# Products that nobody reads, placed where TensorE waits: in the tail of attention and ahead of key-ordered scores

## The chip, the core and the metric

The kernel runs on one core of one Trainium2 chip. The metric is device time in microseconds of one launch, weights in device memory at its start. Engines are named as in the profile: PE (TensorE; PEld is its weight load), DVE (VectorE), ACT (ScalarE), POOL (GpSimd), SP (SyncE, which issues most DMAs).

## What is computed

Two layers, each of gated cross-attention and a gated mixture of experts, on x of 8 x 256 rows of 256 values, with a context of 8 x 120 rows. Each layer has 16 heads of 16, and 8 experts of which every row takes two. Layer 0 has experts of three matrices (hidden width 688, SiLU gate), layer 1 of two (width 256, squared ReLU).

```python
x = x + tanh(g_xattn[l]) * attention_l(layernorm(x), ctx)      # softmax over 120 keys
x = x + tanh(g_ffn[l])   * experts_l(layernorm(x))             # top 2 of 8, weighted
# experts of layer 0: (silu(x @ gate[e]) * (x @ up[e])) @ down[e]
# experts of layer 1: square(relu(x @ w1[e])) @ w2[e]
```

## The kernel before

All engines have instruction lists of their own, written out by hand, and meet at semaphores; each list runs strictly in its order. So a product stands where the code puts it on PE, and what is queued behind it waits with it.

**Attention** of a layer goes over 16 units of 128 query rows (`for u in range(NU)`, two units per batch entry; `at(u)` gives the entry `b`, whether u is even, and whether there is a next entry). PE's list of unit u: `scores(G + 1)` are the query-ordered scores of the next unit (L1254), which DVE reduces to row maxima (L841). Then `shifted(G)`, the key-ordered scores of this unit: L1265, with the row maxima subtracted by the products of L1270. ACT exponentiates them (L647 or L649). Ahead of `shifted(G)` stands a wait for `d_ct`, DVE's transpose of the unit before (L858), since both use bank 4 of PSUM. Then follow `route` (L1312: router logits of an earlier unit), `out_proj` (L1299 and the bias L1300), in even units the query projection of the next entry (L1237), in odd units the transposes of the rows after it (L1231) and `ranks` (L1319 to L1328: each row's place among its expert's rows), `max_t` (L1279), `values` (L1291), and `x2_t` (L1306: transposes of normalized rows for the router).

DVE's `residual` (L875) waits for `out_proj`, and makes the statistics; POOL turns them into mean and reciprocal root (`ln2_rstd`, L514 to L519); ACT applies them (L657); PE transposes the result (L1306); ACT copies it (L663); PE makes the logits. DVE takes the top two (`route1`), PE ranks them, DVE makes the row addresses (`route2`), and POOL scatters the rows to device memory, four indirect DMAs per entry (L544). POOL's list mixes `ln2_rstd` and `scatter`, so that a later statistic waits for the scatters ahead of it.

**The last unit** (u = 15) has no next unit's scores; **the tail** is what then remains: the last two transposes for the router, one output projection, two `ranks`, three `route`.

**The expert stage** goes over 39 blocks of 128 rows. SP loads each block (L398) once the list of full blocks is made (`d_l1`) and the scatters of the first six entries have landed (L402). PE transposes a block (`block_t`, L1468), DVE copies it (L1118), PE multiplies it by the first matrices (`up`, L1482), and after the activation transposes the hidden rows (L1495, L1503) and multiplies by the last matrix (`down`, L1512). POOL scatters the results (L551). Block 0's transposes stand on PE behind the last `ranks`. At the very end DVE combines the results without PE.

The added product reads two constants, `ident_b` (a 128 x 128 identity in bf16) and `sel_rows` (128 x 480 in bf16), and writes bank 7 or 2 of PSUM, which are written anew before they are read next.

Of the kernel before, what the change touches and what calls it, by code (L numbers as in the profile page):

```python
# [27 lines left out]
def need(eng, sem, value):  # L28

    if not isinstance(value, int) or value > 0:  # L30
        eng.wait_ge(sem, value)
# [11 lines left out]
def flamingo_kernel(nc, x, ctx_rows, mask, g_xattn, g_ffn, attn_w, attn_b, router_w, experts, out):  # L43
    NB, S, D = x.shape
    K = ctx_rows.shape[1]
# [6 lines left out]
    NU = NT  # L52
# [22 lines left out]
    with es:  # L75
        def sb(name, shape, dt=F32):
            return es.enter_context(nc.sbuf_tensor(name, shape, dt))
# [122 lines left out]
        sel_rows = sb("sel_rows", [P, 4, K], BF16)  # L200
        ident_b = sb("ident_b", [P, P], BF16)
# [11 lines left out]
        ps = es.enter_context(nc.psum_tensor("ps", [P, 8, 512], F32))  # L213
# [92 lines left out]
        def at(u):  # L306
            return u // 2, u % 2 == 0, u // 2 + 1 < NB

        def run_blocks(l, step):
            for j in range(BLOCKS):  # L310
                step(j, j % U3, j == 0, j == BLOCKS - 1)
# [888 lines left out]
        def _(t):  # L1200
            t.wait_ge(C_id, 2)

            for l in range(2):
# [37 lines left out]
                def scores(G):  # L1241

                    b, qt, f = G % NU // 2, G % 2, G // 2 % 2
                    t.wait_ge(a_q, G // 2 + 1)
                    t.wait_ge(a_k, 4 * l + 2 * (b // 4) + 2)
                    if l == 0:
                        for g in range(4):
                            rows = slice(Q4 * g, Q4 * g + Q4)
                            t.matmul(ps[:, g, 0:4 * K].rearrange("p (j k) -> p j k", j=4), ones[rows, :],
                                     mask3[rows, b:b + 1, :].to_broadcast([Q4, 4, K]), start=True, stop=False)  # L1250
                    for j in range(4):
                        for g in range(4):
                            rows = slice(Q4 * g, Q4 * g + Q4)
                            i = t.matmul(ps[:, g, j * K:(j + 1) * K], qT[rows, f, j // 2, j % 2, qt * P:(qt + 1) * P],  # L1254
                                         kT_all[rows, b, j // 2, :], start=(l == 1), stop=(l == 1 or j == 3))
                    i.then_inc(p_s, 1)
# [17 lines left out]
                def max_t(G):  # L1274

                    for h in range(2):
                        t.wait_ge(d_max[h], G + 1)
                    t.wait_ge(d_part, 2 * G + 2)
                    t.matmul(ps[:, 0, 0:P], m_hi, ident_b[:, :], start=True, stop=True).then_inc(p_m, 1)  # L1279
# [16 lines left out]
                def out_proj(G):  # L1296
                    t.wait_ge(d_c, G + 1)
                    for k in range(KT):
                        t.matmul(ps[:, 1, 0:D], cT[:, G % 2, k, :], w_att[:, 3, k, :], start=(k == 0), stop=False)  # L1299
                    t.matmul(ps[:, 1, 0:D], ones[:, :], bo_rows[:, :], start=False, stop=True).then_inc(p_o, 1)  # L1300

                def x2_t(G):
                    t.wait_ge(a_xn2, G + 1)
                    need(t, a_x2, G)
                    for k in range(KT):
                        i = t.transpose(ps[:, 6, k * P:(k + 1) * P], xn2[:, G % 6, k * P:(k + 1) * P], ident[:, :])  # L1306
                    i.then_inc(p_x2, 1)

                def route(G, bank):
                    t.wait_ge(a_x2, G + 1)  # L1310
                    for k in range(KT):
                        i = t.matmul(ps[:, bank, 2 * P:2 * P + NE], xn2T[:, k, :], wr[:, l, k, :], start=(k == 0), stop=(k == KT - 1))  # L1312
                    i.then_inc(p_lg, 1)

                def ranks(B):

                    t.wait_ge(d_mask, B + 1)
                    need(t, d_cum, 2 * B)
                    t.matmul(ps[:, 3, 0:NE], tri[:, :], maskb[:, 0, :], start=True, stop=False)  # L1319
                    t.matmul(ps[:, 3, 0:NE], ones[:, :], cumb[:, :], start=False, stop=True)  # L1320
                    t.matmul(ps[:, 3, NE:2 * NE], tri[:, :], maskb[:, 1, :], start=True, stop=False)
                    t.matmul(ps[:, 3, NE:2 * NE], ones[:, :], maskb[:, 0, :], start=False, stop=False)
                    i = t.matmul(ps[:, 3, NE:2 * NE], ones[:, :], cumb[:, :], start=False, stop=True)
                    if B % NB in (EARLY - 1, NB - 1):

                        t.matmul(ps[:, 3, 2 * NE:3 * NE], ones[:, :], cumb[:, :], start=True, stop=False)
                        t.matmul(ps[:, 3, 2 * NE:3 * NE], ones[:, :], maskb[:, 0, :], start=False, stop=False)
                        i = t.matmul(ps[:, 3, 2 * NE:3 * NE], ones[:, :], maskb[:, 1, :], start=False, stop=True)  # L1328
                    i.then_inc(p_rk, 1)


                B0, G0 = NB * l, NU * l
                if l == 0:
                    ctx_t(0)
# [55 lines left out]
                for u in range(NU):  # L1390
                    b, even, nxt = at(u)
                    B, G = B0 + b, G0 + u
                    if u + 1 < NU:

                        t.wait_ge(a_m, G + 1)
                        if u >= 2:
                            t.wait_ge(d_o, G - 1)
                        if u >= 4:
                            t.wait_ge(d_lg, G - 3)
                        t.wait_ge(a_xnT, min(B + 2, B0 + NB))  # L1400
                        if even and b >= 3:
                            t.wait_ge(d_rk, B - 2)
                        scores(G + 1)

                    if u >= 1:
                        t.wait_ge(d_ct, G)
                    if u >= 3:
                        t.wait_ge(a_x2, G - 2)
                    if l == 0 and u == 0:
                        t.wait_ge(a_ctx, 4)  # L1410
                        t.wait_ge(d_v, 2)
                    if l == 1 and u == 0:
                        t.wait_ge(d_v, 2 * NB)
                    if l == 0 and u - 1 in FILL_V:
                        t.wait_ge(d_v, FILL_V[u - 1] + 1)
                    if l == 0 and u - 1 in (2, 3):
                        t.wait_ge(a_k, u)
                    shifted(G)
                    if u + 1 < NU:
                        t.wait_ge(d_max[0], G + 2)  # L1420
                    if u >= 3:
                        route(G - 3, 1)
                    if u >= 1:
                        out_proj(G - 1)
                    if u + 1 < NU:
                        t.wait_ge(d_max[1], G + 2)
                    if even and nxt:
                        q_proj(B + 1, 0, 2)
                    if not even and b + 2 < NB:
                        x_t(B + 2, 2)  # L1430
                    if not even and b >= 2:
                        ranks(B - 2)
                    if u + 1 < NU:
                        max_t(G + 1)
                    values(G, 0)
                    if even and nxt:
                        q_proj(B + 1, 1, 3)
                    values(G, 1)
                    if u >= 2:
                        x2_t(G - 2)  # L1440
                    if l == 0 and u in FILL_V:
                        v_proj(B0 + FILL_V[u], 5)
                    if l == 0 and u in (2, 3):
                        k_proj(1, u - 2)
                G1, B1 = G0 + NU - 1, B0 + NB - 1
                route(G1 - 2, 5)
                x2_t(G1 - 1)
                t.wait_ge(d_o, G1)
                t.wait_ge(d_lg, G1 - 2)
                out_proj(G1)  # L1450
                t.wait_ge(d_rk, B1 - 1)
                ranks(B1 - 1)
                route(G1 - 1, 7)
                x2_t(G1)
                route(G1, 0)
                t.wait_ge(d_rk, B1)
                ranks(B1)


                t.wait_ge(d_lg, NU * (l + 1))  # L1460
# [3 lines left out]
                def block_t(j):  # L1464
                    t.wait_ge(L_xg[j % U3], 16 * (uses(l, j) + 1))
                    need(t, e_x, J0[l] + j)
                    for k in range(KT):
                        i = t.transpose(ps[:, 7, k * P:(k + 1) * P], xg[:, j % U3, k * P:(k + 1) * P], ident[:, :])  # L1468
                    i.then_inc(b_x, 1)
# [80 lines left out]
                        down(j, offs[j])  # L1550

                block_t(0)
                run_blocks(l, (blk0, blk1)[l])


# [33 lines left out]
```

## Time and profile before

| | us |
|---|---|
| median of 3 runs | 766.17 |
| lowest and highest | 762.58, 766.7 |
| the profiled execution's own time | 769.0 |
| its span, first to last instruction | 767.3 |
| PE busy in the span | 678.0 (88%) |
| DVE busy | 415.0 (54%) |
| ACT busy | 274.4 (36%) |
| POOL busy | 214.4 (28%) |
| mean granted clock of PE in the span | 0.952 |

Layer 0's attention ends about 154 us into the span, its expert stage runs to about 487, layer 1's attention from there to about 640, its expert stage to about 745. A busy PE may be a slow PE: the granted clock tells at which level it worked, 1.00 for 2.4 GHz and 0.50 for 1.2 GHz.

### The profile page before, as it was taken

How to read it: one execution, taken by the hardware profiler on the slowest of the kernel's cores; microseconds unless marked ns; L12 is line 12 of the kernel's file. 1: busy time of each engine (PE TensorE's matmuls, PEld its weight loads, DVE VectorE, ACT ScalarE, POOL GpSimd, SP SyncE). 2: the span in 40 equal slices, each digit the busy share in tenths (PEclk: the TensorE clock that was granted, in tenths of full speed). 3: DMA queues.
4: the chain of work that ended last, by engine and by line, in shares of the span. 5: the costliest groups of instructions: out<-in, count | busy, mean ns of one | idle time of the engine just before them, and what ended most of it. 6: DMA issues, size and time to landing. Idle time of an engine off the chain costs nothing.

```text
span 767.3 us, 17444 instructions
## 1 busy us (share of the span) xinstructions
PE 678.0 (88%) x5804; PEld 520.4 (68%) x5804; DVE 415.0 (54%) x1385; ACT 274.4 (36%) x528; POOL 214.4 (28%) x399
## 2 busy tenths in 40 slices
PE   5798999859999999999999999978888885999970
PEld 3666767637777777777777777657666663788850
DVE  4777888753333333233332332469989876454426
ACT  3556576411211112112111112256555541354530
POOL 4122553460111111111111011212355436344440
PEclk9999999859999999999999999999999986899995
DMA  9044554461131131111011010320112122544428
GB/s 218 18 144 138 182 179 141 148 220 43 56 101 51 36 79 35 35 32 39 28 35 36 29 28 21 143 92 29 58 64 70 64 85 78 151 125 121 123 83 328
DMA packets 50856, 70.71 MB, mean 92 GB/s; under 512 B 7687, under 2 KB 38023, under 8 KB 50771
## 3 DMA queue, kind: packets, MB, share of 16 engines
q1 hardware_dynamic: 42380, 50.85, 22.1%
q0 software_dynamic: 6816, 18.69, 6.9%
q8 instruction: 51, 0.84, 0.5%
q10 hardware_dynamic: 1575, 0.05, 0.1%
q14 instruction: 34, 0.28, 0.1%
HBM read 46.55 MB, written 23.02 MB: 91 GB/s over the span
## 4 chain that ended last, share of the span: by engine, by line
PE 69%; DVE 18%; issue 5%; DMA 4%; POOL 2%; ACT 2%; DVEq 0%; SPq 0%; POOLq 0%; ACTq 0%
PE ps L1482 28%; PE ps L1512 17%; PE ps L1299 4%; DVE m_rows L841 4%; PE ps L1495 3%; DVE x_sb L825 3%; PE ps L1312 2%; PE ps L1237 2%; DVE ctx_q L858 2%; PE ps L1468 2%; PE ps L1291 2%; DMA ys_dram<-share,dest_i 2%; PE ps L1265 2%; PE ps L1254 1%; DVE x_sb L875 1%
## 5 line engine op out<-in xcount | busy, mean ns | idle before, releaser
L1482 PE MATMUL ps<-w_all,share 128*128 x780 | 232.4, 446 | 4.2 <-DVE share L1118 4.2
L1482 PEld LDWEIGHTS ps<-w_all,share 128*128 128x128 f32 x780 | 146.9, 193 | 66.5 <-issue 8.4
L551 POOL DMA_INDIRECT ys_dram<-share,dest_i x78 | 75.9, 974 | 333.2 <-DVE share L1129 279.8
L1512 PE MATMUL ps<-w_all,share 112*128 (+1 forms) x624 | 147.9, 380 | 1.7 <-ACT share L737 1.0
L1512 PEld LDWEIGHTS ps<-w_all,share 112*128 112x128 f32 (+1 forms) x624 | 112.4, 190 | 15.1 <-issue 2.6
L1145 DVE TENSOR_TENSOR share<-share,ps 128x344 f32<-128x344 f32 x78 | 40.0, 513 | 140.5 <-PE ps L1482 79.3
L726 ACT COPY share<-ps 128x512 f32<-128x512 f32 x39 | 22.9, 587 | 151.9 <-PE ps L1495 151.9
L841 DVE TENSOR_REDUCE m_rows<-ps 128x8 f32<-128x960 f32 x64 | 70.4, 1139 | 11.0 <-PE ps L1254 10.9
L723 ACT ACTIVATE share<-ps 128x344 f32<-128x344 f32 x78 | 35.9, 460 | 106.9 <-PE ps L1482 106.9
L544 POOL DMA_INDIRECT xs_dram<-xn,slot_now x64 | 63.7, 996 | 21.9 <-issue 14.6
L514 POOL TENSOR_SCALAR nm<-mv 128x1 f32<-128x1 f32 (+1 forms) x48 | 12.4, 257 | 162.7 <-DVE mv L881 116.8
L1129 DVE COPY share<-ps 128x256 f32<-128x256 f32 x39 | 16.6, 426 | 68.3 <-PE ps L1512 68.3
L1265 PE MATMUL ps<-q_flat,w_all 32*120 32x256 f32 x512 | 42.1, 413 | 8.2 <-DVE ctx_q L858 6.2
L647 ACT ACTIVATE share<-ps,mask_col 120x1024 f32<-120x1024 f32 x32 | 33.9, 1111 | 26.1 <-PE ps L1270 26.0
L1299 PE MATMUL ps<-w_att,cT 128*128 128x256 f32 x128 | 39.8, 438 | 1.4 <-DVE m_rows L841 0.9
L1115 DVE SCALAR_TENSOR_TENSOR xid<-share,be 128x1 f32<-128x1 f32 x78 | 17.3, 222 | 42.4 <-PE ps L1468 42.0
L1254 PE MATMUL ps<-w_all,q_flat 32*128 32x120 f32 x1024 | 35.6, 275 | 4.9 <-ACT q_flat L629 4.2
L1254 PEld LDWEIGHTS ps<-w_all,q_flat 32*128 32x128 f32 x1024 | 33.1, 186 | 8.3 <-issue 6.6
L1237 PE MATMUL ps<-share,w_att 128*128 128x256 f32 x128 | 34.3, 393 | 3.4 <-issue 2.5
L649 ACT ACTIVATE share<-ps 120x1024 f32<-120x1024 f32 x32 | 31.0, 1020 | 14.3 <-PE ps L1270 14.3
L629 ACT ACTIVATE q_flat<-ps,bq,qs 128x256 f32<-128x256 f32 x64 | 32.5, 565 | 8.9 <-PE ps L1237 8.8
L1468 PEld LDWEIGHTS ps<-ident,share 128*128 128x128 f32 x156 | 22.5, 146 | 15.8 <-issue 2.6
(202 smaller groups left out, 991.3 us busy)
## 6 DMA issues: line engine op xcount, KB each, us to landing
share<-xs_dram SPq DMA_DIRECT2D x78, 129.0 KB, 2.1
w_all<-ys_dram SPq DMA_DIRECT2D x16, 512.0 KB, 7.2
w_all<-gate SPq DMA_DIRECT2D x8, 688.0 KB
w_all<-up SPq DMA_DIRECT2D x8, 688.0 KB
w_all<-down SPq DMA_DIRECT2D x8, 560.0 KB
w_all<-w SPq DMA_DIRECT2D x16, 256.0 KB
xs_dram<-q_flat SPq DMA_DIRECT2D x17, 129.0 KB, 2.4
out<-x_sb SPq DMA_DIRECT2D x8, 256.0 KB, 5.6
```

The costliest lines, as they stand in the source:

```text
L544: g.indirect_dma_start(xs_dram, bass.IndirectOffsetOnAxis(ap=slot_now[:, B % 2, t, k:k + 1], axis=0), xn2[:, s + t, :], None).then_inc(sca ...
L551: g.indirect_dma_start(ys_dram, bass.IndirectOffsetOnAxis(ap=dest_i[:, u:u + 1], axis=0), y_sb[:, u, :], None).then_inc(D_y[u], 16)
L723: a.activation(act_sb[:, 344 * q:344 * q + 344], ps[:, 2 * q, 0:344], ACT.Silu).then_inc(e_act, 1)
L841: v.tensor_reduce(m_part[:, 2 * h:2 * h + 2, 0:4], ps[:, 2 * h:2 * h + 2, 0:4 * K].rearrange("p g (j k) -> p g j k", j=4), X, ALU.max).the ...
L1145: v.tensor_tensor(h_sb[:, 344 * q:344 * q + 344], act_sb[:, 344 * q:344 * q + 344], ps[:, 2 * q + 1, 0:344], ALU.mult).then_inc(e_h, 1)
L1237: i = t.matmul(ps[:, bank, 0:S], w_att[:, 0, k, m * P:(m + 1) * P], xn1T[:, k, :], start=(k == 0), stop=(k == KT - 1))
L1254: i = t.matmul(ps[:, g, j * K:(j + 1) * K], qT[rows, f, j // 2, j % 2, qt * P:(qt + 1) * P], kT_all[rows, b, j // 2, :], start=(l == 1), s ...
L1265: t.matmul(ps[0:K, 4 + g, 2 * m * P:2 * (m + 1) * P].rearrange("p (e q) -> p e q", e=2), kT_all[rows, b, m, :], qT[rows, f, m, :, qt * P:( ...
L1299: t.matmul(ps[:, 1, 0:D], cT[:, G % 2, k, :], w_att[:, 3, k, :], start=(k == 0), stop=False)
L1468: i = t.transpose(ps[:, 7, k * P:(k + 1) * P], xg[:, j % U3, k * P:(k + 1) * P], ident[:, :])
L1482: i = t.matmul(ps[:, bank, 0:w], xgT[:, k, :], w_all[:, bass.ds(off + (k * UPW[l] + col - EW[l]), w)], start=(k == 0), stop=(k == KT - 1))
L1512: i = t.matmul(ps[:, 6, 0:D], hT[0:r, c + KD[1] * (j % 2) * l, :], w_all[0:r, bass.ds(off + (KT * UPW[l] + c * D - EW[l]), D)], start=(c = ...
```

## The change

A helper `idle_products(n, bank)` issues n products whose result nobody reads. It is called in the last unit of both layers (six, ahead of the wait for `d_ct`), in layer 1's even units from u = 2 (two at the same place), at eight places of each layer's tail, and between block 0's transposes and its first expert products. The helper waits for nothing and raises no semaphore. Nothing is taken away.

```diff
+                def idle_products(n, bank):
+                    for _ in range(n):
+                        t.matmul(ps[:, bank, 0:4 * K], ident_b[:, :], sel_rows[:, :, :].rearrange("p j k -> p (j k)"),
+                                 start=True, stop=True)
...
                         scores(G + 1)
 
+                    if u == NU - 1:
+                        idle_products(6, 7)
+                    elif l == 1 and even and u >= 2:
+                        idle_products(2, 7)
                     if u >= 1:
                         t.wait_ge(d_ct, G)
...
                 G1, B1 = G0 + NU - 1, B0 + NB - 1
+                idle_products(2, 2)
                 route(G1 - 2, 5)
+                idle_products(3, 2)
                 x2_t(G1 - 1)
                 t.wait_ge(d_o, G1)
                 t.wait_ge(d_lg, G1 - 2)
+                idle_products(1, 2)
                 out_proj(G1)
                 t.wait_ge(d_rk, B1 - 1)
                 ranks(B1 - 1)
                 route(G1 - 1, 7)
+                idle_products(15, 2)
                 x2_t(G1)
+                idle_products(2, 2)
                 route(G1, 0)
                 t.wait_ge(d_rk, B1)
+                idle_products(6, 2)
                 ranks(B1)
+                idle_products(5, 2)
...
                 block_t(0)
+                idle_products(3, 2)
                 run_blocks(l, (blk0, blk1)[l])
```

PE's list at the last unit and the tail of layer 1 (layer 0's reads the same). L1335 is the added product; L1306 transposes normalized rows, L1312 makes logits, L1265 and L1270 are key-ordered scores, L1299 and L1300 the output projection.

```order
 L1291 MATMUL ps<-share,w_all 32x128 x16
 L1306 MATMUL ps<-ident,xn 128x128 x2
+L1335 MATMUL ps<-sel_rows,ident_b 128x480 x6
 L1265 MATMUL ps<-q_flat,w_all 120x256 x4
 L1270 MATMUL ps<-share,sel_rows 120x128 x8
```

```order
-L1306 MATMUL ps<-ident,xn 128x128 x2
-L1312 MATMUL ps<-wr,share 128x8 x2
+L1335 MATMUL ps<-sel_rows,ident_b 128x480 x15
+L1306 MATMUL ps<-ident,xn 128x128 x2
+L1335 MATMUL ps<-sel_rows,ident_b 128x480 x2
+L1312 MATMUL ps<-wr,share 128x8 x2
+L1335 MATMUL ps<-sel_rows,ident_b 128x480 x6
 L1319 MATMUL ps<-maskb,tri 128x8
 L1320 MATMUL ps<-cumb,ones 128x8
```

The first piece puts six products between the transposes that end unit 14 and the last unit's key-ordered scores. In the second the pair L1306, L1312 stands as before, with 15 products ahead of it, 2 within and 6 behind it, ahead of the last `ranks`.

PE's list in an even unit of layer 1 (L1254 are the query-ordered scores of the next unit):

```order
 L1306 MATMUL ps<-ident,xn 128x128 x2
 L1254 MATMUL ps<-w_all,q_flat 128x120 x16
+L1335 MATMUL ps<-sel_rows,ident_b 128x480 x2
 L1265 MATMUL ps<-q_flat,w_all 120x256 x4
 L1270 MATMUL ps<-share,sel_rows 120x128 x8
```

Two products come between the two kinds of scores. The lists of DVE, ACT and SP are the same as before, and POOL's too.

## Rows read from the trace of the kernel before

**Rows 1.** The page, section 2: granted clock in 40 equal slices, tenths.

```profile
PEclk9999999859999999999999999999999986899995
```

**Rows 2.** Windows, engine PE: stretch, length, PE busy (instructions), granted clock, DMA share, GB/s.

```profile
144.00:150.70 6.70, 6.63 (x65) 0.50 0.02 5
...
563.80:567.10 3.30, 1.77 (x37) 1.00 0.02 5
...
580.80:584.20 3.40, 2.13 (x59) 1.00 0.02 5
...
625.20:628.60 3.40, 1.66 (x39) 1.00 0.72 232
...
635.50:642.20 6.70, 3.63 (x34) 1.00 0.18 63
642.30:659.30 17.00, 10.55 (x37) 0.50 0.46 131
```

**Rows 3.** Timeline, PE, units 13 and 14 of layer 1: start, duration, operation [idle before].

```profile
617.26 1.11 PE L1299 MATMUL ps<-w_att,cT 128*128 128x256 f32 x4
...
618.21 0.27 PE L1300 MATMUL ps<-bo_rows,ones 128*128 128x256 bf16 x1
...
621.16 0.71 PE L1265 MATMUL ps<-q_flat,w_all 32*120 32x256 f32 x8
...
622.28 0.29 PE L1270 MATMUL ps<-share,sel_rows 32*120 32x128 bf16 x8
```

**Rows 4.** Timeline, PE, unit 15 of layer 1.

```profile
628.41 1.06 PE L1265 MATMUL ps<-q_flat,w_all 32*120 32x256 f32 x8 [1.74 <-DVE ctx_q L858]
...
630.77 1.02 PE L1312 MATMUL ps<-wr,share 128*128 128x8 f32 x4
...
631.65 2.05 PE L1299 MATMUL ps<-w_att,cT 128*128 128x256 f32 x4
...
633.49 0.42 PE L1300 MATMUL ps<-bo_rows,ones 128*128 128x256 bf16 x1
```

**Rows 5.** Timeline, PE, L1312 in units of layer 1: odd, even, odd, even.

```profile
584.45 0.61 PE L1312 MATMUL ps<-wr,share 128*128 128x8 f32 x4 [0.86 <-DVE m_rows L841]
...
591.08 0.61 PE L1312 MATMUL ps<-wr,share 128*128 128x8 f32 x4 [0.71 <-DVE m_rows L841]
...
600.73 0.61 PE L1312 MATMUL ps<-wr,share 128*128 128x8 f32 x4 [0.86 <-DVE m_rows L841]
...
608.80 0.61 PE L1312 MATMUL ps<-wr,share 128*128 128x8 f32 x4 [0.59 <-DVE m_rows L841]
```

**Rows 6.** Groups of instructions by form: busy, mean ns | idle before.

```profile
L1249 PE MATMUL ps<-mask,ones 32*128 32x480 bf16 x64 | 6.1, 370 | 4.0 <-ACT share L621 1.5 <-ACT q_flat L629 1.2 <-ACT share L637 0.6
```

**Rows 7.** Timeline, PE, tail and first blocks of layer 1.

```profile
644.40 0.69 PE L1306 MATMUL ps<-ident,xn 128*128 128x128 f32 x2 [4.27 <-ACT xn L657]
...
645.54 1.02 PE L1312 MATMUL ps<-wr,share 128*128 128x8 f32 x4 [0.46 <-ACT share L663]
...
648.20 0.17 PE L1319 MATMUL ps<-maskb,tri 128*128 128x8 bf16 x1 [1.63 <-issue]
...
648.97 0.66 PE L1468 MATMUL ps<-ident,share 128*128 128x128 f32 x2 [0.41 <-issue]
...
650.43 2.07 PE L1482 MATMUL ps<-w_all,share 128*128 x4 [0.80 <-DVE share L1118]
...
660.36 1.03 PE L1482 MATMUL ps<-w_all,share 128*128 x4
...
662.52 1.03 PE L1482 MATMUL ps<-w_all,share 128*128 x4
```

**Rows 8.** Layer 0: a piece of the chain that ended last, then PE's timeline.

```profile
157.00 5.26 DMA xs_dram<-xn,slot_now
...
165.85 0.66 PE L1468 MATMUL ps<-ident,share 128*128 128x128 f32 x2 [1.52 <-DMA share<-xs_dram]
...
167.33 6.82 PE L1482 MATMUL ps<-w_all,share 128*128 x16 [0.81 <-DVE share L1118]
```

## The prediction

> **What bounds the kernel now.** I read the page first: its line of granted clock is 9s except at a few slices [rows 1], in a span of 767.3 us. The profiled execution's own time is 769.0 us, 2.8 us above the median of 766.17. PE works 88% of the span, so the question is at which level of its clock. The windows view over both layers gives the answer [rows 2]. From 144.0 to 150.7 the granted clock is 0.50 (1.2 GHz instead of 2.4), and PE is busy 6.63 us of 6.70: this is the last unit of layer 0's attention. Unit 15 of layer 1 runs the same way [rows 4]. Each layer also has a stretch of 17 us at 0.50 from the attention's tail into the first expert blocks: layer 1's row is here, layer 0's shows in rows 8. Ahead of the fall at 628.6, PE was busy 1.66 us of 3.40. Two short falls lie in odd units of layer 1. Ahead of one PE was busy 1.77 us of 3.30; in the next odd unit, with the same operations and 2.13 of 3.40, nothing fell [rows 2]. So the clock falls behind stretches in which PE waited much, and of units that are alike one is hit and another not.
>
> **What a fall costs.** Units 13 and 14 of layer 1 run at the full level [rows 3], unit 15 at half [rows 4]. Key-ordered scores: 621.16 to 622.57, 1.41 us, against 628.41 to 630.77, 2.4 us: 1.0. Router product L1312: 0.61 [rows 5] against 1.02: 0.4. Output projection L1299: 1.11 against 2.05: 0.9. Bias L1300: 0.27 against 0.42: 0.15. Together **2.5 us**, and nothing hides them: VectorE's residual waits for L1300, and from it go statistics, POOL's reciprocal root and POOL's four scatters, whose end sets when the last normalized rows reach PE. A short fall costs, from one L1312 to the next, 608.80-600.73 = 8.07 against 591.08-584.45 = 6.63: 1.4 us [rows 5].
>
> **The change part by part.** It adds 100 products and removes nothing: 12 in the last units, 14 in layer 1's even units, 74 in the two tails. All other engines keep their order. Each streams 480 bf16 columns. No row shows one back to back. L1249 has the same width and type, 370 ns on average [rows 6]; L1300 with 256 columns takes 0.27 [rows 3]. The difference is 0.10 us per 224 columns, or 0.45 ns a column, so 480 cost 0.21 us each where products are pipelined. That is the low end; the high end is 0.37 us each, if nothing overlaps. I take 0.21, since four L1299 of 256 f32 columns start 0.95 us ahead of what follows [rows 3], so PE does pipeline. At half clock it is some 0.4.
>
> *Last unit, six ahead of L1265.* 6 x 0.21 = 1.3 us in an idle of 1.74 [rows 4]: hidden. The products then stand in most of the idle that lies ahead of the fall, so I take it that the unit stays at full speed: **-2.5** in layer 1, and the same taken for layer 0, whose stretch is alike.
>
> *Layer 1's even units, two each.* They do not stand in the idle: in an even unit scores and key-ordered scores follow each other. The 0.42 us delay the latter, and the 0.71 us that PE then waits for the row maxima ahead of the L1312 at 591.08 [rows 5] take it up. ScalarE gets its scores 0.4 later, and has time. Cost 0 (0.4 x 7 = 2.9 if that cover is gone). Gain 0 too: the falls come in the odd units, where no product is added.
>
> *Tail.* In layer 1 PE waits 4.27 us for L1306 [rows 7]: fifteen products take 3.15 (5.6 at the high price, 1.3 too long). Two stand in the idle of about half a microsecond ahead of L1312, six (1.3) in the 1.63 ahead of L1319. Five (1.05) stand where only 0.41 was idle ahead of block 0's transposes: PE is 0.6 late there, but VectorE, which copies the block next, still has the routing to end after L1319, so I charge 0.1 and keep 0.6 for the range. Three (0.6) before the first expert products fit in 0.80. One ahead of the last output projection delays it by 0.2; POOL is then still in its scatters, so nothing. With the clock held, L1306 (0.69, about 0.25 less) and L1312 (1.02, 0.4 less) are shorter, and both are on the path. Then the blocks: 650.43 to 660.36 is 9.93 us for three at half clock, and the next takes 662.52-660.36 = 2.16 [rows 7]; 3 x 2.16 = 6.48, so **-3.45**. Layer 1: -2.5 -0.65 +0.1 -3.45 = -6.5.
>
> Layer 0's expert stage begins otherwise: its first block waits for a load, which waits for the scatter's landing, 5.26 us after the issue at 157.00; PE idles 1.52 us for it and starts at 165.85 [rows 8]. That chain starts at the same residual, so it moves by 2.5; the faster L1306 and L1312 bring nothing. The first sixteen expert products start at 167.33 and run at half until 171.2, 3.9 us, of which half is saved: **-1.95**; block 0's transposes save 0.2. Layer 0: -4.65. Five products fill 1.05 of the 1.52 idle.
>
> After this PE is without idle in the expert stages, so what is gained ahead lasts. Sum: -11.15, and +0.5 for small delays where products fill an idle to its end (three before L1306, of 0.6 us). 766.17 - 10.65 = **755.5**. The median run may have fewer short falls than the profiled execution (2 x 1.4 would be its 2.8 us); they stay as they are before and after.
>
> The Trainium skill (TensorE: Matmul & The Clock Gate, Part 1 on the HAM clock gate) says the monitor is free-running against the kernel, so that the same kernel changes level at other places from run to run. The trace agrees in that like odd units differ. By it, each run of before and after has its own number of short falls, 1.4 us each, which widens the range.
>
> **Rivals.**
> 1. *Slower: the products run at half clock.* If they do not hold the clock, fifteen take 6.0 against 4.27: +1.7; two +0.3, six 2.4 against 1.63: +0.8, five 2.0 against 0.41: +1.6, three 1.2 against 0.80: +0.4. That is +4.8 in layer 1 and about +4 in layer 0, where the load hides part: 775. It decides once a product takes over 0.28 us (4.27/15). For: products follow long idle, in which the clock falls today. Against: from 635.5 to 642.2 the clock was at 1.00 [rows 2], and the fifteen begin in that stretch. 0.05.
> 2. *One fall comes back.* Idle is left in the tail: about 1.1 us after the fifteen, and in layer 0 between five products and the load. One of the two block starts is then at half again: 2 to 3.45 given back, 757.5 to 759. 0.16.
> 3. *The gain is taken up later.* If layer 0's scatter landing stays (the DMA queues are busy there with the last expert's weights), 2.5 is lost: 758. If products also cost the high price, another 2 to 3 in the tails: 761. 0.12, of it 0.05 within 0.5%.
> 4. *The even units' products stop the short falls.* Then up to 2.8 more than summed: 753. Against: they stand a unit away from the idle. 0.07.
> 5. *The falls matter less than their stretches.* Only one place may be on the path, -3.5: 763, within 0.5%. 0.02. The Trainium skill (the same page, Part 1) puts the warm-up penalty under 1% of a typical span; by that the gain would end at 7.7 us, 758.5, in the range of the second rival. The terms above, all from rows, come to more than that.
>
> **How the numbers follow.** The forecast has 0.58, own range 753 to 758. With rivals 2, 4 and most of 3 the range is 751 to 762. Over 0.5% faster (about what a measurement of this kernel can tell from no change) is under 762.3: 0.58 + 0.16 + 0.07 + 0.07 = 0.88. Within 0.5%: 0.07. Slower: 0.05.
>
> **What would show it.** Granted clock 1.00 from the start of both last units through the first expert blocks; L1265 of unit 15 in 0.7 us and not 1.06; the new products 0.2 us apart, ending before the waits they stand in; layer 1's first blocks 2.16 us apart; layer 0's first sixteen expert products in 4.63; short falls in odd units still possible, and even units unchanged in length. A stretch at 0.50 behind the fifteen products, or an idle of PE at L1306 that is gone because the products are late, would make it wrong.

## The result and the profile after

| | before | after |
|---|---|---|
| median, us | 765.32 (4 runs) | 756.21 (4 runs) |
| lowest and highest | 762.58, 766.7 | 754.82, 756.57 |
| the profiled execution's own time | 769.0 | 756.57 |
| its span | 767.3 | 754.8 |
| PE busy in the span | 678.0 (88%) | 684.7 (91%) |
| mean granted clock of PE | 0.952 | 0.985 |

The ratio after to before is 0.9865 with a 95% interval of 0.9827 to 0.9902: by it the change is 10.3 us faster (7.5 to 13.2). It is not the quotient of the medians, which lie 9.1 us apart. The measured 756.21 is inside the range, 0.7 us from the forecast, and in the case that had 0.58. (Each layer's 37 products behind the last unit stand at eight places: seven in the tail and the one behind block 0's transposes.)

The page of after, its first line and the line of granted clock that stood in [rows 1]:

```profile
span 754.8 us, 17644 instructions
...
PEclk9999999999999999999999999999999999999995
```

PE is busy 6.7 us more than before in a span that is 12.5 shorter: the products are work, put in time in which PE would mostly have waited. Of the 8s, the 6 and the two 5s of [rows 1] only the 5 at the end is left: DVE's last combination, in which PE has no work.

The windows of after on PE, over both last units, the tails and the first blocks (length, PE busy, granted clock, DMA share, GB/s):

```profile
142.80:144.70 1.90, 1.39 (x8) 1.00 0.64 208
144.70:151.00 6.30, 6.24 (x92) 1.00 0.12 22
151.10:163.10 12.00, 9.82 (x61) 1.00 0.72 246
163.20:170.00 6.80, 6.13 (x25) 1.00 0.60 186
...
575.90:578.70 2.80, 1.85 (x36) 1.00 0.00 0
578.90:582.10 3.20, 3.20 (x19) 0.50 0.05 10
622.20:628.70 6.50, 6.23 (x92) 1.00 0.04 13
628.80:641.30 12.50, 10.38 (x64) 1.00 0.34 107
641.40:648.00 6.60, 5.35 (x28) 1.00 0.61 182
```

The four long stretches at 0.50 of before, two last units and two tails with their first blocks, now read 1.00. One short fall is left, at 578.8, in an odd unit of layer 1, where no product stands.

Layer 1's last unit, its tail and its first blocks, in PE's timeline (start, duration, operation, idle before), against [rows 4, 7]:

```profile
620.39 1.38 PE L1335 MATMUL ps<-sel_rows,ident_b 128*128 128x480 bf16 x6
622.27 0.71 PE L1265 MATMUL ps<-q_flat,w_all 32*120 32x256 f32 x8 [0.51 <-DVE ctx_q L858]
...
624.08 1.11 PE L1299 MATMUL ps<-w_att,cT 128*128 128x256 f32 x4
...
631.33 3.20 PE L1335 MATMUL ps<-sel_rows,ident_b 128*128 128x480 bf16 x15
635.74 0.44 PE L1306 MATMUL ps<-ident,xn 128*128 128x128 f32 x2 [1.21 <-ACT xn L657]
636.01 0.57 PE L1335 MATMUL ps<-sel_rows,ident_b 128*128 128x480 bf16 x2
...
637.10 1.38 PE L1335 MATMUL ps<-sel_rows,ident_b 128*128 128x480 bf16 x6
638.94 0.18 PE L1319 MATMUL ps<-maskb,tri 128*128 128x8 bf16 x1 [0.47 <-DVE maskb L910]
...
639.16 1.17 PE L1335 MATMUL ps<-sel_rows,ident_b 128*128 128x480 bf16 x5
640.17 0.38 PE L1485 MATMUL ps<-ident,share 128*128 128x128 f32 x2
...
641.35 1.13 PE L1499 MATMUL ps<-w_all,share 128*128 x4 [0.19 <-DVE share L1118]
...
643.43 1.13 PE L1499 MATMUL ps<-w_all,share 128*128 x4 [0.73 <-DVE share L1118]
```

(L1485 and L1499 are the transposes of a block and the first expert products, L1468 and L1482 of before.) Read the idles in brackets. The products before L1265 take 1.74 down to 0.51, and those before L1306 4.27 down to 1.21. Fifteen take 3.20, six 1.38, five 1.17. The last of each group's time is what one takes alone, 0.37, so the pitch is (3.20-0.37)/14 = 0.20. L1265 takes 0.71, not 1.06; L1299 1.11, not 2.05. The first expert products of one block and the next stand 2.08 apart, where three blocks took 9.93.

The same in layer 0, where block 0 waits for a load (here L1485 has no wait that the view shows), against [rows 8]:

```profile
161.72 1.17 PE L1335 MATMUL ps<-sel_rows,ident_b 128*128 128x480 bf16 x5
162.95 0.41 PE L1485 MATMUL ps<-ident,share 128*128 128x128 f32 x2
...
164.17 4.89 PE L1499 MATMUL ps<-w_all,share 128*128 x16 [0.21 <-DVE share L1118]
```

Where the 12.5 us between the two profiled spans went: from L1265 of the last unit to the first expert products layer 0 took 167.33-144.07 = 23.26 and now 164.17-144.70 = 19.47, **-3.8**; layer 1 took 650.43-628.41 = 22.02 and now 641.35-622.27 = 19.08, **-2.9**. From there to the last of the first-matrix products, layer 0's expert stage goes from 312.24 to 310.31, **-1.9**, and layer 1's from 88.74 to 85.38, **-3.4**. The stretch from layer 0's last first-matrix product to L1265 of layer 1's last unit goes from 148.84 to 147.79, **-1.05**: it has one short fall of the clock and no longer two. Ahead of all this, L1265 of layer 0's last unit starts 0.6 later than before (144.70 against 144.07). These come to the 12.5.

### The profile page after: what moved, and what is told of

Read it like the earlier page. It is cut to its first block, busy times and chain, and to the rows that moved or that the text cites. A ratio compares the mean times of both kernels' runs of the same rounds, so it can differ in the third digit from the quotient of the medians.

```text
span 754.8 us, 17644 instructions
## 1 busy us (share of the span) xinstructions
PE 684.7 (91%) x5904; PEld 517.5 (69%) x5904; DVE 414.9 (55%) x1385; ACT 273.9 (36%) x528; POOL 213.0 (28%) x399
## 3 DMA queue, kind: packets, MB, share of 16 engines
q0 software_dynamic: 6816, 18.69, 7.0%
## 4 chain that ended last, share of the span: by engine, by line
PE 72%; DVE 16%; issue 5%; DMA 3%; POOL 2%; ACT 2%; DVEq 0%; POOLq 0%; SPq 0%; ACTq 0%
PE ps L1499 28%; PE ps L1529 17%; PE ps L1299 4%; PE ps L1512 3%; DVE m_rows L841 3%; DVE x_sb L825 3%; PE ps L1237 2%; PE ps L1312 2%; PE ps L1485 2%; PE ps L1265 2%; PE ps L1291 2%; PE ps L1254 2%; DVE ctx_q L858 2%; PE ps L1215 1%; DVE x_sb L875 1%
## 5 line engine op out<-in xcount | busy, mean ns | idle before, releaser
L1499 PE MATMUL ps<-w_all,share 128*128 x780 | 227.6, 439 | 2.7 <-DVE share L1118 2.7
L1499 PEld LDWEIGHTS ps<-w_all,share 128*128 128x128 f32 x780 | 144.2, 190 | 63.4 <-issue 5.2
L1265 PE MATMUL ps<-q_flat,w_all 32*120 32x256 f32 x512 | 40.6, 401 | 5.7 <-DVE ctx_q L858 3.7
L1254 PE MATMUL ps<-w_all,q_flat 32*128 32x120 f32 x1024 | 35.6, 275 | 4.9 <-ACT q_flat L629 4.2
L1254 PEld LDWEIGHTS ps<-w_all,q_flat 32*128 32x128 f32 x1024 | 33.1, 186 | 8.3 <-issue 6.6
L649 ACT ACTIVATE share<-ps 120x1024 f32<-120x1024 f32 x32 | 31.0, 1020 | 17.8 <-PE ps L1270 17.8
L1299 PE MATMUL ps<-w_att,cT 128*128 128x256 f32 x128 | 36.5, 409 | 0.3 <-DVE m_rows L841 0.2
L825 DVE SCALAR_TENSOR_TENSOR x_sb<-w_all,wcomb,x_sb 128x256 f32<-128x256 f32 x64 | 26.0, 477 | 13.1 <-DMA w_all<-ys_dram 13.1
```

Source lines behind the costliest of these rows:

```text
L825: v.scalar_tensor_tensor(out=xt, in0=yg[:, b, t, k, :], scalar=wcomb[:, 2 * b + t, k:k + 1], in1=xt, op0=ALU.mult, op1=ALU.add).then_inc(d ...
L1265: t.matmul(ps[0:K, 4 + g, 2 * m * P:2 * (m + 1) * P].rearrange("p (e q) -> p e q", e=2), kT_all[rows, b, m, :], qT[rows, f, m, :, qt * P:( ...
L1499: i = t.matmul(ps[:, bank, 0:w], xgT[:, k, :], w_all[:, bass.ds(off + (k * UPW[l] + col - EW[l]), w)], start=(k == 0), stop=(k == KT - 1))
```

## The experiments

What was open: whether the clock alone explains the gain, which places bring it, whether even units' products do anything, and whether more or other products would bring more. Nine kernels were run, three of them on two chips, in three groups, each on one chip and beside runs of the kernel before on the same chip. Ratios are to those, and a gain in us is worked out from the ratio.

### First group: a chip on which the kernel before takes 798 us

**The changed kernel again**, with no edit.

> The changed kernel once more, beside the runs of this call. If short falls of the clock hit like units by chance, its time spreads by about 1.4 us from run to run around 756, and one to two short falls in odd units of layer 1 may show, at other units than the one fall at 578.8 us of the first trace. If the places of the falls are fixed by the program, the fall stands at the same unit again.

Measured: 792.21 (8 runs) against 798.33 of the kernel before (25 runs, 796.86 to 802.9); ratio 0.9912 [0.988, 0.9944]. There is a gain here too; it reads smaller, though the interval overlaps that of the result. Neither theory on the spread could be read from this, since both kernels are over 30 us slower than in the result above, and the windows of this run say where. In order: layer 0's attention, its expert stage, layer 1's attention:

```profile
0.00:182.80 182.80, 145.81 (x2043) 0.97 0.47 144
182.90:495.00 312.10, 311.64 (x1371) 0.99 0.14 43
495.10:678.80 183.70, 152.46 (x2025) 0.96 0.22 73
```

Layer 0's expert stage is as long as in the kernel before, 312 us, and not 310.3 as in after. The attention stages, up to the first expert products, are 182.8 and 183.7 long, where after's take 164.2 and 166.9. Its waits (sum, count, longest):

```profile
ACT share L647 <- remote: 24.0, 5, 6.1
DVE x_sb L875 <- remote: 20.9, 8, 2.7
```

With four more of ACT at L649, these are 17 single waits of up to 6.1 us on ACT and DVE; "remote" says that the trace puts them down to nothing on this core. No profile of the result and of the other groups has such a line. Their cause wasn't tried. What matters here is that PE is then idle for long at places that the change doesn't fill. Ahead of layer 0's first expert products it stands still for 4.83 us:

```profile
182.83 6.92 PE L1499 MATMUL ps<-w_all,share 128*128 x16 [4.83 <-issue]
```

The granted clock is 0.50 from 180.1 to 187.0 there, and again from 678.5 to 685.3, at layer 1's first blocks. So on this chip the tails' products did not keep the first blocks at full speed, and that part of the gain is missing.

**Even units' products out.**

```diff
-                    elif l == 1 and even and u >= 2:
-                        idle_products(2, 7)
```

> The fourteen products in layer 1's even units are left out. Theory (they stand away from the idle that precedes a fall): same time as the changed kernel, 756 within 1, L1312 of even units waits 0.6 to 0.7 us again where it now waits 0, and a distance of 6.63 from odd to even L1312 either way. Rival (they prevent short falls): two or more short falls in each run, 1.4 to 2.8 slower than the changed kernel.

Measured: 801.11 (12 runs), ratio 1.0027 [1.0004, 1.0049]. That is 8.9 us above the changed kernel on this chip, against a theory of none.

**Products in odd units instead.** Three each in units 5, 7, 9 and 11, where PE waits for DVE.

```diff
-                    elif l == 1 and even and u >= 2:
-                        idle_products(2, 7)
+                    elif l == 1 and u in (5, 7, 9, 11):
+                        idle_products(3, 7)
```

> The fourteen products of the even units are taken out, and three stand instead ahead of L1265 in units 5, 7, 9 and 11 of layer 1, where PE waits 0.67 us for DVE. Theory (a fall needs the idle just ahead of it): three times 0.2 us fits in the 0.67, no short fall in layer 1's odd units in any run, so 755.0, up to 1 us less than the changed kernel, and with less spread. Rival (the short falls come from something else than PE's idle): a short fall still shows in some runs, same time and spread as the changed kernel.

Measured: 794.97 (12 runs), ratio 0.996 [0.9936, 0.9984]: 2.8 us above the changed kernel and not below it, and short falls show all the same (at 600.2 and 610.4).

**Narrow products.** All 100 stay where they are, but stream 8 columns, not 480.

```diff
-                        t.matmul(ps[:, bank, 0:4 * K], ident_b[:, :], sel_rows[:, :, :].rearrange("p j k -> p (j k)"),
+                        t.matmul(ps[:, bank, 0:8], ident_b[:, :], sel_rows[:, 0, 0:8],
```

> All 100 products stay in their places, but each streams 8 columns instead of 480. Theory (what counts is that PE streams through the idle): the clock falls again in both last units and both tails as in the kernel before, and the time is that of before, 763 to 767. Rival (that PE's queue holds instructions at those places is enough, or that the products delay something to its advantage): the clock stays up and the time is 755 to 757.

Measured: 804.42 (8 runs), ratio 1.0059 [1.0034, 1.0084]: no gain at all, and half a per cent worse than the kernel before, which stays unexplained.

Taken alone these four say that the even units' products are worth 1.1%, against "cost 0, gain 0". The clock points the same way: its mean over a run is 0.953 to 0.964 in the twelve runs without them and has a median of 0.968 with them. In the two profiled executions layer 1's attention, counted from layer 0's last first-matrix product to the last unit's L1265, has 20.6 us at half and takes 164.41 without them, and has 13.6 at half and takes 160.43 with them. But the profile without them also has stretches at half in layer 0 (at 27.6 and 153.9), where the edit changes nothing, and the waits of this chip open falls in many places. So the questions were put again on other chips.

### Second group: one part of the change alone

The kernel before takes 768.03 here (19 runs).

**Only the last units' six products**: the even units' and all 74 behind the last units are left out.

> Only the six products of each last unit stay; those of the tails and of the even units are gone. Theory (two separate gains): the last unit of each layer runs at full speed, 2.5 us less per layer against the kernel before, the clock then falls in the tail's long idle and the first blocks run at half as before: 5 us less than before, 760 where before is 765. Rival (the six only put the fall off): the fall comes later in the same unit or right at the tail and the gain is under 2 us.

Measured: 762.08 (10 runs), ratio 0.9945 [0.9913, 0.9976], 4.2 us (1.8 to 6.7). The prediction had 2 x 2.5. Its windows show the last units at 1.00 and both tails at 0.50, some 17 us each, as expected:

```profile
144.00:151.00 7.00, 5.40 (x88) 1.00 0.15 32
153.60:170.40 16.80, 8.80 (x28) 0.50 0.58 186
625.00:632.00 7.00, 5.52 (x89) 1.00 0.07 23
634.90:651.70 16.80, 8.64 (x31) 0.50 0.44 134
```

**Only the tails' products**: those of the last units and of the even ones are left out.

```diff
-                    if u == NU - 1:
-                        idle_products(6, 7)
-                    elif l == 1 and even and u >= 2:
-                        idle_products(2, 7)
```

> Only the products of the tails stay (74 of 100). Theory: the last units fall to half in most runs and lose their 2.5 us per layer, the tails and first blocks hold the full level: about 6 us less than before, 759 where before is 765, and the two halves together make the whole change's 10 to 12. Rival (entering the tail at half, the fifteen products take 0.4 us each and delay it): the time is that of before or up to 4 us more.

Measured: 761.52 (10 runs), ratio 0.992 [0.9888, 0.9952], 6.1 us (3.7 to 8.6). The terms of the tails in the prediction come to 0.65 - 0.1 + 3.45 + 1.95 + 0.2 = 6.15, less 0.5. The windows are the other half of the picture:

```profile
144.70:151.30 6.60, 6.60 (x69) 0.50 0.01 3
151.50:168.00 16.50, 13.11 (x93) 1.00 0.65 217
623.00:630.00 7.00, 5.29 (x115) 1.00 0.37 116
630.10:646.00 15.90, 13.49 (x87) 1.00 0.30 92
```

Layer 0's last unit is at half, both tails at full. Layer 1's last unit is at full in this execution without any product: the same unit, with the same idle ahead (1.72 us here, 1.74 before), is hit in one run and not in another.

So there are two places, and each set of products keeps the clock up behind itself: both tails fell with the last units' products alone, and layer 0's last unit fell with the tails' alone. The gains, 4.2 and 6.1 against 10.3 for the whole, fit together, but each is known to 2.5 us only (by the medians 5.9 and 6.5 against 9.1), so the sum proves little. In layer 0 they are not quite independent. With the last unit fast alone, the first expert products start at 164.36 and no longer at 167.33, but the stretch at half still lasts until 170.5 (171.2 before): more of them run at half, and the stage is 313.37 long against 312.24. One microsecond of what the last unit gains is lost again as long as the tail isn't filled.

**Even units' products out, again.** The same edit as before, on this chip.

> The kernel without the even units' products once more, beside the next one, since the first look at it fell on a chip with waits of several us that no kernel here causes. Theory: without such waits it is within 1 us of the changed kernel. Rival: 1.4 to 2.8 slower, by more short falls in layer 1.

Measured: 758.2 (4 runs), ratio 0.9885 [0.9826, 0.9944]. Layer 1's attention has one short fall, at 596.5.

**Products in odd units instead, again.**

> Products in units 5, 7, 9 and 11 instead of the even ones, once more for the same reason. Theory: no short fall in layer 1, 0 to 1.5 us less than the kernel without both. Rival: short falls as without them, same time.

Measured: 756.81 (4 runs), ratio 0.9872 [0.9816, 0.9928]. Neither is to be told from the other or from the changed kernel's 0.9865. In the profiled execution of the last, whose span is 755.7 us, no stretch is at 0.50 until the end of the kernel. PE's timeline at one of its odd units:

```profile
543.64 0.78 PE L1335 MATMUL ps<-sel_rows,ident_b 128*128 128x480 bf16 x3
544.38 0.71 PE L1265 MATMUL ps<-q_flat,w_all 32*120 32x256 f32 x8
```

The three products end where PE used to wait for DVE, 0.67 us in an odd unit of after, and L1265 follows with no idle at all.

### Third group: other numbers and widths

The kernel before takes 768.22 here (13 runs).

**Narrow products, again.**

> The 100 products at 8 columns instead of 480 once more, for the same reason as the two before. Theory (PE must stream through the idle): both last units and both tails fall to half, time of the kernel before within 0.5%. Rival (instructions in PE's queue are enough): granted clock 1.00 there and a time 1.2% less than before.

Measured: 767.84 (10 runs), ratio 0.9999 [0.9969, 1.0028]: the whole gain is gone. All 100 products are in the same places, and the clock falls in layer 0's last unit (145.5 to 152.3) and in both tails, whose windows are below. Layer 1's last unit, which the theory had at half too, ran at full in this execution: its L1265 takes 0.71, behind an idle of 1.59 and six narrow products.

```profile
159.30:172.70 13.40, 8.01 (x41) 0.50 0.59 185
637.10:657.40 20.30, 12.50 (x78) 0.50 0.40 120
```

In its timeline of layer 1 the fifteen are there and done in half a microsecond, behind which PE is idle for 2.79 us:

```profile
640.53 0.54 PE L1335 MATMUL ps<-sel_rows,ident_b 128*128 128x8 bf16 x15
```

So it is neither the instructions nor their order that brings the gain, but the time for which they keep PE working. The Trainium skill (TensorE: Matmul & The Clock Gate, Part 1) ties the clock to how busy the array has been recently; in that, the trace agrees.

**Thirty for fifteen** before the last L1306.

```diff
-                idle_products(15, 2)
+                idle_products(30, 2)
```

> Thirty products instead of fifteen ahead of L1306 in each tail. Theory: they take 0.20 us each, so 15 more are 3.03 us, of which the 1.2 to 1.3 us of idle left there take up a part; L1306 waits 0 instead of 1.3, and each layer is 1.7 to 1.8 us longer: 3.5 us more than the changed kernel in all. Rival (what follows has slack, since POOL's scatters and the block loads end later anyway): under 1 us more.

Measured: 758.88 (4 runs), ratio 0.9882 [0.9859, 0.9906]. PE's timeline in layer 1:

```profile
630.79 6.24 PE L1335 MATMUL ps<-sel_rows,ident_b 128*128 128x480 bf16 x30
636.86 0.38 PE L1306 MATMUL ps<-ident,xn 128*128 128x128 f32 x2
```

Thirty take 6.24 and PE has no wait left: L1306 is late. From L1265 of the last unit to L1306, layer 0 takes 15.14 against 13.61 of after and layer 1 15.13 against 13.47, 3.2 more in both together, near the 3.5 of the theory. Whether the kernel takes 3.5 us more or under 1 is not settled by the times: the median is 2.7 above after's, on another chip, and the ratio 0.17% (1.3 us) above, within both intervals. The profiled spans are 754.9 and 754.8, since this execution has no short fall in layer 1's attention and after's has one. Thirty bring the clock nothing that fifteen don't, and delay the next step.

**The five ahead of block 0's transposes out.**

```diff
                 ranks(B1)
-                idle_products(5, 2)
```

> The five products behind the last ranks are left out. Theory: block 0's transposes start 0.2 (layer 0, then at the load's landing) to 0.8 us (layer 1) earlier, VectorE follows by 0.2 to 0.3 in each layer, and the clock stays up by the six and the three around them: 0.5 us less than the changed kernel. Rival (the five hold the clock in layer 0, where block 0 waits for its load): a fall at about 164 us in some runs, 2 us more in these.

Measured: 757.28 (4 runs), ratio 0.988 [0.9819, 0.9941]. The median can't be told from the changed kernel's, but the profile differs. Windows and timeline of layer 0 (here L1484 transposes the block, L1498 is the first expert product):

```profile
160.00:163.60 3.60, 1.65 (x17) 1.00 0.51 165
163.80:167.00 3.20, 3.20 (x7) 0.50 0.59 151
```

```profile
163.14 0.41 PE L1484 MATMUL ps<-ident,share 128*128 128x128 f32 x2 [1.49 <-DMA share<-xs_dram]
```

PE waits 1.49 us for the load, as it did 1.52 in [rows 8], and the clock is at half from 163.7 to 167.1, over the first expert products. Layer 0's expert stage takes 311.67 against 310.31, so this fall costs 1.4. It is the second rival of the prediction, "one fall comes back", and it came in the one profiled execution without the five; in the five of groups two and three that keep five or three of them and the rest of the tail, nothing fell there. In layer 1, where no load is waited for, nothing fell without them either, and its way from L1265 to the first expert products takes 18.69 us against 19.08 of after: there the five cost 0.4.

**Five to three, and the odd units' products.**

```diff
-                    elif l == 1 and even and u >= 2:
-                        idle_products(2, 7)
+                    elif l == 1 and u in (5, 7, 9, 11):
+                        idle_products(3, 7)
...
-                idle_products(5, 2)
+                idle_products(3, 2)
```

> Products in units 5, 7, 9 and 11 instead of the even units, and three instead of five behind the last ranks. Theory: no fall of the clock before the end of the second expert stage, and 0.2 us less per layer than with five: the least of all kernels here, 755. Rival: nothing that can be told from the changed kernel.

Measured: 758.47 (4 runs), ratio 0.9871 [0.9846, 0.9895]: no better, and not told from the changed kernel, as the rival had it. Both attentions are at 1.00 but for one short stretch at 26.8, and a fall stands in a place that no theory had, in layer 1's expert stage:

```profile
673.00:677.80 4.80, 3.30 (x19) 1.00 0.45 141
678.90:682.10 3.20, 3.20 (x11) 0.50 0.29 82
```

```profile
678.44 1.37 PE L1499 MATMUL ps<-w_all,share 128*128 x3 [2.14 <-DVE share L1118]
```

PE waits 2.14 us for DVE's copy. DVE itself waits for results to land in device memory. Its wait in layer 1's expert stage (641 to 745), first of this run, then of the changed kernel (sum, count, longest):

```profile
DVE dest_i L1124 <- DMA ys_dram<-share,dest_i: 9.8, 5, 3.5
```

```profile
DVE dest_i L1124 <- DMA ys_dram<-share,dest_i: 5.3, 3, 2.4
```

With a wait of 9.8 us the stage takes 89.43 here, with 5.3 it takes 85.38 in the changed kernel. In the second run without even units' products the same wait came to 11.4 us, and that expert stage took 89.89, with a fall at 681.8, at the end of an idle of 2.40. Where the clock holds at its start, the length of this stage goes with that wait. Whether the edits have a part in it isn't shown, and what makes a landing late wasn't tried.

**The same stretches in all profiles of the result and of groups two and three**, in us, from the starts of the products. "Way" is from L1265 of a layer's last unit to the first expert products, "stage" from there to the last first-matrix product, "between" from that of layer 0 to L1265 of layer 1's last unit, with the number of short falls in it.

| | way 0 | stage 0 | between (falls) | way 1 | stage 1 |
|---|---|---|---|---|---|
| before | 23.26 | 312.24 | 148.84 (2) | 22.02 | 88.74 |
| after | 19.47 | 310.31 | 147.79 (1) | 19.08 | 85.38 |
| last units' six only | 19.95 | 313.37 | 147.51 (1) | 19.51 | 86.98 |
| tails' only | 23.06 | 310.32 | 148.16 (1) | 19.08 | 84.98 |
| even units' out | 20.45 | 310.31 | 147.89 (1) | 19.10 | 89.89 |
| odd units instead | 20.41 | 310.32 | 145.99 (0) | 19.09 | 86.60 |
| narrow | 22.82 | 312.78 | 149.82 (2) | 20.85 | 86.87 |
| thirty for fifteen | 20.69 | 310.31 | 146.12 (0) | 20.58 | 84.39 |
| five out | 19.88 | 311.67 | 147.70 (1) | 18.69 | 85.20 |
| odd units, three for five | 19.89 | 310.32 | 146.64 (0) | 18.69 | 89.43 |

Layer 0's stage says whether the clock held: 310.31 or 310.32 where it did, 1.4 to 3.1 more where it fell. Between the layers the length goes by the number of short falls, some 1.5 us for each.

## Why the prediction was right, point by point

**The last unit, -2.5 a layer: right for a run that is hit.** From L1265 to the last L1306, layer 0 took 16.11 and now takes 13.61, layer 1 took 15.99 and now 13.47: 2.5 in both. As a term of the median it is too large. Of the three profiles without wide products ahead of the last unit (before, tails' only, narrow), all three have layer 0's last unit at half and only one, the one that the prediction was read from, layer 1's. Alone the two bring 4.2 us [1.8, 6.7] against 5.0, after layer 0 has lost one microsecond again in its first blocks.

**The price of a product: right.** 0.21 was worked out from rows of 256 and 480 columns, and 0.20 measured. The high end, 0.37, is what one takes alone and never the pitch. With it rival 1, which decides at 0.28, is out: the fifteen ran at a granted clock of 1.00.

**Even units at cost 0: right. Gain 0: open, with signs against it.** From the odd to the even L1312 it was 591.08-584.45 = 6.63 [rows 5]; after, with two products between, it is the same:

```profile
561.97 0.61 PE L1312 MATMUL ps<-wr,share 128*128 128x8 f32 x4 [0.86 <-DVE m_rows L841]
...
568.60 0.61 PE L1312 MATMUL ps<-wr,share 128*128 128x8 f32 x4
```

568.60-561.97 = 6.63, and the wait of 0.71 before the even L1312 is gone, as the prediction had it: the delay is taken up whole. The stretch between the layers says the same: without a short fall it is 146.12 with the even units' products and 145.99 without. On their gain the chips disagree: 0.9885 without them against 0.9865 with them, inside each other's intervals, in the second group and the result; 1.0027 against 0.9912, clear of each other's intervals, in the first group, among waits that nothing explains. Rival 4, that they stop the short falls, is neither shown nor out. They don't stop all: one stands at 578.8 in after, another at 580.1 in the run without the five. But the three profiles of the table with them have two short falls between the layers, the five without wide products in even or odd units have seven. With products in the odd units, where the idle is, the two profiles of the later groups have none; on the chip of the first group there were two. At 1.4 a fall this is too little to show in four runs.

**Tail of layer 1, -0.65 and +0.1: about right, the five under-priced.** L1265 to the first expert products moved by 2.94, against 2.5 + 0.65 - 0.1 = 3.05. The five cost 0.4 there (19.08 with them, 18.69 without or with three), where I had charged 0.1 and kept 0.6; block 0's transposes, 0.66 before and 0.38 now, gave most of it back, which the sum had left out for layer 1.

**Blocks, -3.45: right.** The first three blocks of layer 1 took 9.93 and now take 6.42: 3.51. That the whole stage is 3.36 shorter is no proof, since it varies by 5.5 us over the profiles in which the clock held at its start. Layer 0's **-1.95: right**, 1.93. (The sixteen products now take 4.89; the 4.63 that the prediction gave as a sign doesn't follow from its own 6.82 - 1.95 = 4.87.)

**Layer 0's way to the first products: right, and a microsecond of chance.** The terms were -2.5 and -0.2; measured -3.8 in after. "That chain starts at the same residual, so it moves by 2.5" holds for the chain up to the scatters. From the last scatter's issue to SP's load issue was 163.31-157.00 = 6.31 before and is 160.28-155.00 = 5.28 after: the landing came a microsecond sooner than a pure shift. In after the load no longer ends the chain. PE's five products do:

```profile
161.87 1.03 PE ps L1335 x5
...
162.95 0.43 PE ps L1485 x2
```

But the products don't make the landing earlier: with the same products in layer 0, the runs without the even units' and with the odd units' have 6.23 and 6.19 for that step, wait for the load behind the five as the prediction had it, and their way is 2.8 shorter, against the forecast's 2.7. This is the run without the even units' (L1483 transposes the block):

```profile
164.29 0.41 PE L1483 MATMUL ps<-ident,share 128*128 128x128 f32 x2 [1.05 <-DMA share<-xs_dram]
```

So the step depends on when the scatter lands in a given run. What moves that landing wasn't tried.

**"After this PE is without idle in the expert stages, so what is gained ahead lasts": wrong for layer 1.** In layer 0 it holds: the stage's length moved by the clock's term alone. In layer 1 the stage is 84.39 to 89.89 us long in runs whose clock at its start is the same, by DVE's waits for landings and the idle that they make on PE. The run with the odd units' products and three for five lost 4 us there against after, more than its attention had gained. That it did not spoil this forecast is luck of a kind: after's stage is among the short ones, and a gain of a microsecond ahead of it can't be counted on.

**The small delays, +0.5**, stand for the three before L1306, of 0.6 us: in layer 1 PE still waits 0.18 us behind them, so they cost nothing.

**The number.** The terms were read from a profile at 769.0 and taken from a median of 766.17. Between the two profiles 12.5 went, against 10.65: 5.7 in layer 0's way and stage against 4.65, most of it the early landing, 6.3 against 6.5 in layer 1's, 1.05 for a short fall fewer, which the prediction named as chance and not as gain, and no small delays; 0.6 was lost ahead of layer 0's last unit. The medians lie 9.1 apart, the ratio says 10.3. So the mechanism was right; that the forecast is off by only 0.7 is in part luck, with a layer 1 term that few runs have in full and a last stage that varies by more than that.

**Rivals.** 2 came true in the run without the five, in one layer, and with all products on the chip of the first group, in both; not in the result. 3: what was gained ahead was not taken up in layer 0, and in layer 1 only in other runs. 5: both places are on the path, as the two partial kernels show. The bound of 7.7 us that stands with it is below the medians' 9.1 and the ratio's 10.3, but the interval reaches down to it.

## What to carry to other kernels

Where PE waits at a fixed place and what follows runs at half clock for long, wide products that nobody reads can stand in the wait: count the wait, divide by the pitch, and leave a remainder, since products beyond the wait delay the next step by nearly their whole time (thirty for fifteen: 3.0 us more of them in a wait of 1.2 to 1.3 left, the next step 1.5 and 1.7 us later in the two layers). Look for it by the granted clock of the stretch *behind* the wait, put products only where that stretch is on the path, and price it by the same operations at the other level. The instructions alone don't do it: the same hundred with 8 columns brought nothing.

## What the runs showed that I had not expected

- One chip takes 798 us for the kernel whose medians are 765 to 768 on the others, with single waits of up to 6.1 us on ACT and DVE in the attention stages. A change that fills known idles leaves PE's new, longer ones open there, and both first blocks fell to half again.
- Where the short falls stand differs from run to run of nearly the same kernel: 578.8 in after, 580.1 without the five, 596.5 without the even units', 598.6 with only the tails', 549.4 with only the last units', and between 26.8 and 30.6 in three kernels of the later groups, in layer 0's early attention, which none of them changes. One profile can't tell whether an edit stopped one.
- A fall can come inside an expert stage in which PE works above 90% otherwise, at a single wait of 2.14 or 2.40 us; the profile of before has none there.
